# Slots of the first experts named by one-hot matmuls, rows gathered by token and results added into x

## What is computed

```
h = layernorm(x) * (1 + ca) + sa ;  x = x + ga * mamba(h)                 # layer 0, state-space scan
h = layernorm(x) * (1 + cb) + sb
w, idx = top_k(h @ Wr, 2) ;  w = softmax(w)                               # 8 experts, no capacity limit
x = x + gb * sum_k w_k * (silu(h @ W1[idx_k]) * (h @ W3[idx_k])) @ W2[idx_k]
h = ... ;  x = x + ga' * attention(h)                                     # layer 1, 8 heads, causal
h = ... ;  x = x + gb' * experts1(h)                                      # 16 experts, top 2, capacity 640
```

## Time and profile before

| | us |
|---|---|
| median of 3 runs | 3121.29 (3119.28 to 3121.49) |
| the profiled execution | 3119.1 |
| its span, first to last instruction | 3117.0 |
| TensorE busy | 2633.4 (84%) |
| VectorE busy | 2089.7 (67%) |
| GpSimd (POOL) busy | 1148.6 (37%) |
| ScalarE busy | 1157.2 (37%) |

### The profile page before, as it was taken

One profiled execution on the slowest core, in us unless ns is written; L12 is line 12 of the kernel. 1 busy time (PEld: TensorE's weight loads), 2 busy tenths in 40 slices (PEclk: granted clock), 3 DMA queues, 4 the chain that ended last, 5 costly groups with the idle time before them and its releaser, 6 DMA issues. The chain is left out here.

```text
span 3117.0 us, 37717 instructions
## 1 busy us (share of the span) xinstructions
PE 2633.4 (84%) x11376; PEld 1725.6 (55%) x11377; DVE 2089.7 (67%) x4427; ACT 1157.2 (37%) x2271; POOL 1148.6 (37%) x494
## 2 busy tenths in 40 slices
PE   6788888888877508999399999999999999929998
PEld 3233333343333505777267767766777777727776
DVE  4999999999998501222377758784777577535554
ACT  4556566656643202222133413341344143201111
POOL 1798898898896160000210001020102000224444
PEclk8899999999998558999699999999999999959999
DMA  4455555654553522111300000010000000024553
GB/s 152 170 165 166 181 171 153 188 174 150 188 182 108 208 95 88 59 60 57 114 21 8 1 18 18 1 35 22 15 1 28 14 1 1 28 97 110 130 129 69
DMA packets 148491, 278.70 MB, mean 89 GB/s; under 512 B 16060, under 2 KB 101868, under 8 KB 147692
## 3 DMA queue, kind: packets, MB, share of 16 engines
q1 hardware_dynamic: 127052, 238.85, 24.0%
q0 software_dynamic: 20736, 35.80, 5.1%
q10 hardware_dynamic: 544, 2.10, 0.2%
HBM read 210.03 MB, written 62.47 MB: 87 GB/s over the span
## 5 line engine op out<-in xcount | busy, mean ns | idle before, releaser
L678 POOL TENSOR_TENSOR dbx<-u,b_all 128x2048 f32<-128x2048 f32 x128 | 578.3, 4532 | 105.5 <-DVE u L752 51.6
L418 PE MATMUL y_ps<-hc,ident 128*128 128x512 f32 x768 | 403.7, 642 | 119.8 <-DVE hc L832 118.9
L571 ACT ACTIVATE da_ps<-delta,a_neg 128x512 f32<-128x512 f32 x512 | 346.2, 688 | 322.8 <-DVE hc L832 316.9
L1577 POOL DMA_INDIRECT at_y<-outs,slot_of x64 | 63.0, 984 | 820.3 <-DVE x L1862 457.9
L1822 ACT COPY at_pt<-at_pt_ps 128x512 f32<-128x512 f32 (+3 forms) x384 | 171.3, 481 | 505.5 <-PE at_pt_ps L1712 504.1
L418 PEld LDWEIGHTS y_ps<-hc,ident 128*128 128x128 f32 x768 | 139.4, 198 | 346.8 <-DVE hc L832 250.9
L1608 POOL DMA_INDIRECT slots<-at_r_rows,slot_of x64 | 64.3, 1004 | 672.9 <-DVE slot_of L1960 654.6
L1724 PE MATMUL at_o_ps<-at_pt,at_v 128*128 128x128 f32 x2304 | 299.9, 276 | 2.9 <-DVE at_attn L2034 2.9
L1701 PE MATMUL at_s_ps<-at_qk 128*128 128x512 f32 (+3 forms) x768 | 292.4, 491 | 5.0 <-DVE at_v L2010 3.1
L1724 PEld LDWEIGHTS at_o_ps<-at_pt,at_v 128*128 128x128 f32 x2304 | 277.5, 192 | 11.6 <-issue 11.3
L1812 ACT ACTIVATE at_probs<-at_s_ps,at_small 128x128 f32<-128x128 f32 (+7 forms) x256 | 191.5, 748 | 232.6 <-DVE at_small L2021 232.4
(11 more groups left out here) (291 smaller groups left out, 4659.3 us busy)
## 6 DMA issues: line engine op xcount, KB each, us to landing
b_all<-bc_rows SPq DMA_DIRECT2D x128, 512.0 KB, 4.6
c_all<-bc_rows SPq DMA_DIRECT2D x128, 512.0 KB, 5.2
e_w<-L_ffn_w SPq DMA_DIRECT2D x32, 512.0 KB, 5.3
slots<-zeros SPq DMA_DIRECT2D x40, 260.0 KB, 6.1
e_xs<-slots SPq DMA_DIRECT2D x16, 650.0 KB, 7.2
slots<-zeros SPq DMA_DIRECT2D x24, 384.0 KB, 6.3
w<-L_ffn_W SPq DMA_DIRECT2D x24, 384.0 KB, 8.9
e_xs<-slots SPq DMA_DIRECT2D x72, 128.0 KB, 2.0
```

The costliest lines, as they stand in the source:

```text
L418: mm = nc.tensor.matmul(y_ps[par][:], sh.ident[:], hc[:, at % RING_H, :], start=False, stop=last)
L571: nc.scalar.activation(da_ps[s % RING_DA][:], delta[:, c % 2, m, :], ACT.Exp, scale=sh.a_neg[:, m, n:n + 1]).then_inc(S["da_ready"], 1)
L678: nc.gpsimd.tensor_tensor(dbx[:, at % RING_DBX], pair, rows, ALU.mult).then_inc(S["dbx_ready"], 1)
```

## The change

Routing no longer moves rows to slots. The normalised rows are stored to DRAM by token (`rows0`, 4096 rows of 256 values and four numbers: token number plus one, two weights, first expert). To know which token sits in each slot, the kernel builds one-hot matrices from the slot number: its lane (slot modulo 128) and its tile (slot divided by 128, 72 of them), the latter multiplied by the token number. The sum over tokens of lane x tile products is a matmul, whose result is a 128 x 72 table of tokens. The first experts gather their rows with this table, scale the result by weight and gate, and add it to x in DRAM (`sums0`), where the mamba phase has stored x. The attention loads x back. Its constants are loaded during the first experts. `slots0`, `outs0`, their zero fills (24 pieces of 384 KB) and the attention's fetches and combines are gone; 24 tiles' combine work leaves the attention's loops, 8 tiles' leaves its start.

```diff
 # mamba, SP
-                rows, n, tiles = (d["slots0"], g, 3) if g < FILL0 // 3 else (d["slots1"], g - FILL0 // 3, 2)
+            def store_x(c):
+                sp.wait_ge(S["out_added"], (c + 1) * 2)
+                sp.dma_start(rows, sh.x[:, c * CT:(c + 1) * CT]).then_inc(sh.x_stored, 16)
+                    if c and i == GC - 3:
+                        store_x(c - 1)
             ...
+            store_x(CHUNKS - 1)          # last instruction of SP in the phase
 # routing, SP
-                    sp.dma_start(h_rows[:, bass.ds(b * TPB + th * CT, CT), :], row8[...])
+                    rows = d["rows0"][bass.ds(b * T + th * CH, CH), 0:E].rearrange("(j p) e -> p j e", p=P)
+                    sp.dma_start(rows, row8[:, th * CT:(th + 1) * CT, :]).then_inc(rows_copied[th], 16)
             ...                          # after the expert weights
+            sp.wait_ge(meta_ready, 1)
+                sp.dma_start(d["rows0"][:, E:].rearrange("(t p) c -> p t c", p=P), meta[:]).then_inc(meta_stored, 16)
 # routing, POOL
-            for i in range(TILES):
-                for k in range(2):
-                    nc.gpsimd.indirect_dma_start(out=d["slots0"], ..., in_=h_rows[:, i, :], in_offset=None)
+            for b in range(B):
+                pool.wait_ge(block_hot, b + 1)
+                nc.gpsimd.tensor_tensor(hot_block[:, b % 2], hot_block[:, b % 2], of_token(b), ALU.mult).then_inc(block_set, 1)
 # routing, PE
+            for b in range(B):
+                pe.wait_ge(lane_hot, b + 1)
+                pe.wait_ge(block_set, b + 1)
+                for k in range(2):
+                    for j in range(TPB):
+                        last = nc.tensor.matmul(held_ps[:], hot_lane[:, b % 2, k, j, :], hot_block[:, b % 2, k, j, :], ...)
+                last.then_inc(held_done, 1)
 # routing, VectorE (after the slots; four operations turn slot into lane_of and block_of)
+            for b in range(B):
+                if b >= 2:
+                    dve.wait_ge(held_done, b - 1)
+                nc.vector.tensor_tensor(hot_block[:, b % 2], wide(block_of, b, TILES0), every(block_at, TILES0), ALU.is_equal)
+                nc.vector.tensor_tensor(hot_lane[:, b % 2], wide(lane_of, b, P), every(lane, P), ALU.is_equal)
+            dve.wait_ge(held_done, B)    # then eight operations on 128x72: gather_i, add_i, later
 # first experts, POOL
+            def gather(j):
+                if j >= U:
+                    pool.wait_ge(x_turned, j - U + 1)
+                    pool.wait_ge(weight_chain, 2 * (j - U + 1))
+                nc.gpsimd.indirect_dma_start(out=xs[:, j % U, :], out_offset=None, in_=d["rows0"], in_offset=...gather_i[:, j:j + 1])
+            def add(j):
+                pool.wait_ge(y_copied, j + 1)
+                if j:
+                    pool.wait_ge(added, j * 16)
+                nc.gpsimd.indirect_dma_start(out=d["sums0"], out_offset=...add_i[:, j:j + 1], in_=ys[:, j % U, :],
+                                             in_offset=None, compute_op=ALU.add).then_inc(added, 16)
+            AHEAD, BEHIND = 3, 3
+            for j in range(TILES0 + BEHIND):
+                if j + AHEAD < TILES0:
+                    gather(j + AHEAD)
+                if j >= BEHIND:
+                    add(j - BEHIND)
 # first experts, VectorE: body of tile j
                 multiply(j, r)
+                read_weight(j, r, q)     # 2 operations on 128x1
+                gate_rows(j, r)          # 3 chained operations on 128x256
+                if exists(j - 2):
+                    scale_y(j - 2, (r - 2) % U)   # frees y_ps; waits for added of tile j - 6
 # first experts, ScalarE: copy_y is gone
 # first experts, SP: after the first gather has landed, loads of mods (two), gate weights, positions, output weights
 # attention, SP
+                sp.dma_start(sh.x[:, at], d["sums0"][th * CH:(th + 1) * CH, :]...).then_inc(x_first[th], 16)   # two halves of batch 0
+                sp.dma_start(sh.x[:, b * TPB:(b + 1) * TPB], rows_in).then_inc(S["x_in"], 16)                  # batches 1 to 3
 # attention, POOL: fetch is gone.  VectorE: combine becomes stats (a wait and bn_stats)
```

More of the change, by code:

```diff
@@ L36 @@
 TILES0 = SLOTS0 // P
+META = 4
+ROW = E + META
 HEADS, DH = 8, 128
@@ L952, in _ @@
                 sp.dma_start(sh.w2_0[:, e], d["L0_ffn_W2"][e].rearrange("(m p) f -> p m f", p=P)).then_inc(sh.e0_w_in, 16)
+            sp.wait_ge(meta_ready, 1)
+            with nc.allow_non_contiguous_dma(reason="four numbers a row"):
+                sp.dma_start(d["rows0"][:, E:].rearrange("(t p) c -> p t c", p=P), meta[:]).then_inc(meta_stored, 16)
+            for th in range(CPB):
+                sp.wait_ge(rows_copied[th], 16 * B + 1)
+            sp.wait_ge(meta_stored, 16)
         @block.gpsimd
@@ L1033, in _ @@
             nc.tensor.matmul(tot_ps[:], ones[:], both[:], start=True, stop=True).then_inc(ranked, 1)
+            for b in range(B):
[3 more added lines that the diff above has]
+                    for j in range(TPB):
+                        last = nc.tensor.matmul(held_ps[:], hot_lane[:, b % 2, k, j, :], hot_block[:, b % 2, k, j, :],
+                                                start=(b == 0 and k == 0 and j == 0), stop=(b == B - 1 and k == 1 and j == TPB - 1))
+                last.then_inc(held_done, 1)
         @block.vector
@@ L1123, in phase_experts0, with tiles @@
         assert TILES0 % U == 0
-        def tiles(eng, body):
-            for r in range(U):
-                body(r, r, 0)
-            with eng.Fori(1, LOOPS - 1) as q:
+        def tiles(eng, body, apart=1):
+            for j in range(apart * U):
+                body(j, j % U, j // U)
+            with eng.Fori(apart, LOOPS - 1) as q:
                 for r in range(U):
@@ L1243, in body @@
                     copy_x(j + 1, (r + 1) % U)
-                if exists(j - 2):
-                    copy_y(j - 2, (r - 2) % U, q - (1 if r < 2 else 0))
-            for r in range(U):
-                act.sem_inc(y_out[r], 1)
             copy_x(0, 0)
             tiles(act, body)
-            copy_y(TILES0 - 2, U - 2, LOOPS - 1)
-            copy_y(TILES0 - 1, U - 1, LOOPS - 1)
         @block.vector
@@ L1266, in multiply, with read_weight, gate_rows, scale_y @@
                 nc.vector.tensor_tensor(prod[:, r % 2], act_h[:, r % 2], g_ps[r % 2][:], ALU.mult).then_inc(prod_done, 1)
+            def read_weight(j, r, q):
+                dve.wait_ge(x_in[r], q * 16 + 16)
+                if not early(j, U):
+                    dve.wait_ge(y_copied, j - U + 1)
+                at = weight[:, r:r + 1]
+                nc.vector.scalar_tensor_tensor(out=at, in0=xs[:, r, E + 3:E + 4], scalar=sh.owner[:, bass.ds(j, 1)], in1=xs[:, r, E + 1:E + 2],
+                                               op0=ALU.is_equal, op1=ALU.mult).then_inc(weight_chain, 1)
+                dve.wait_ge(weight_chain, j * 2 + 1)
+                nc.vector.tensor_tensor(at, at, xs[:, r, E + 2:E + 3], ALU.add).then_inc(weight_chain, 1)
+            def gate_rows(j, r):
+                for b in range(1, B):
+                    before = sh.mods[:, 2, 0, :] if b == 1 else gate_row[:, r, :]
+                    if b > 1:
+                        dve.wait_ge(gate_chain, j * (B - 1) + b - 1)
+                    nc.vector.scalar_tensor_tensor(out=gate_row[:, r, :], in0=sh.mods[:, 1, b, :], scalar=sh.later[:, b - 1, bass.ds(j, 1)], in1=before,
+                                                   op0=ALU.mult, op1=ALU.add).then_inc(gate_chain, 1)
+            def scale_y(j, r):
+                dve.wait_ge(y_done, j + 1)
+                dve.wait_ge(gate_chain, (j + 1) * (B - 1))
+                dve.wait_ge(weight_chain, (j + 1) * 2)
+                if not early(j, U):
+                    dve.wait_ge(added, (j - U + 1) * 16)
+                nc.vector.scalar_tensor_tensor(out=ys[:, r], in0=y_ps[:], scalar=weight[:, r:r + 1], in1=gate_row[:, r, :],
+                                               op0=ALU.mult, op1=ALU.mult).then_inc(y_copied, 1)
             def body(j, r, q):
@@ L1611, in _ @@
             for b in range(B):
-                if b + 1 < B:
-                    for j in range(TPB):
-                        fetch((b + 1) * TPB + j)
                 if b > 0:
```

232 lines of the change are left out of this document (121 added, 111 removed).

## The result

The change made the kernel faster: 3043.3 us (median of four runs, 3041.4 to 3044.7) against 3120.3 us of the kernel before beside it (3116.1 to 3121.5). The ratio is 0.9755, 95% interval 0.9738 to 0.9772. I had said 3095 with a range of 3036 to 3130: the direction and the range held, the size did not, 77 us against 25. The profiled execution spans 3039.7 us.

| point | before | forecast | after |
|---|---|---|---|
| first experts' first instruction | 1169.22 | 1114.9 | 1115.31 |
| TensorE's first matmul there | 1180.08 | 1120.9 | 1123.37 |
| first accumulating add issued | | 1138.5 | 1140.39 |
| last add issued | | 1507.7 | 1467.43 |
| attention's first instruction | 1509.45 | 1517.0 | 1476.98 |

What follows compares the result with a forecast made beforehand. Two seams, POOL's routing scatters and the gap before the attention, were the bound. From 3119.1 us, 7.6 more up to the attention, 27.3 less at its start and 5.9 less in its loops gave 3093.5, said as 3095, range 3036 to 3130.

Steps and rivals of the forecast that it cites:

- Bound and seams: Routing's 64 POOL scatters and the gap before the attention's first row are the bound that the change attacks.
- Routing: Routing phase: token table ready at 1111.4, 2 us for stores, 1.5 for the phase change, first experts start at 1114.9.
- my 28.4: One-hot work in routing: VectorE's compares and POOL's multiplies one after the other, plus last matmuls, 28.4 us; 18.5 in parallel.
- rival (d): Routing: the store of four numbers a token is the wall, ending at 1131, 20 us more, 3115 us; chance 6%.
- The loop: First experts: the chain of accumulating adds, 5.20 us a tile over TensorE's 4.42, sets the phase; attention starts at 1517.0.
- Their cycle: First experts, one add to the next: issue 1.56, DMA start 0.50, DMA work 1.30, next start 1.84, together 5.20 us.
- 1.84: First experts: from an add's DMA activity ending to the next add's start, 1.36 - 0.29 + 0.77 us.
- (a): First experts: an add's start is hidden in the wait, cycle 4.72 us, 34 us less, 3061 us; chance 23%.
- (b): First experts: landing is quick enough that TensorE or VectorE keeps the pace, about 4.45 us, 3042 us; chance 11%.
- Rival (c): First experts: the gather on POOL's queue delays the adds, cycle 5.75 us, 39 us more, 3134 us; chance 17%.
- VectorE in the loop: First experts: VectorE needs 4.3 us a tile, up to 5.0, just inside TensorE's 4.42.
- Attention's loops: Attention: 24 combines leave VectorE and count only where TensorE waits, at most 5.9 us gained over three batches.

Runs made afterwards that it cites:

- experiment 5: Changed kernel with the one-hot table in bf16, the token number in two parts multiplied in by ScalarE instead of POOL: 3028.6 us.
- experiment 2: Changed kernel with odd tiles' adds into a second tensor, not added up: 3030.4 us; or with plain scatters, still chained, into an unread tensor: 3025.7 us.
- experiment 3: Changed kernel with a POOL memset of 640, 1 or 1120 elements between the wait and each add: 3054.6, 3049.2 and 3084.8 us.
- experiment 4: Changed kernel with the attention's weights loaded behind the third gather: 3046.7 us; or with its constants loaded in the attention again: 3049.8 us.
- experiment 1: Changed kernel with the attention's four old VectorE operations a tile on scratch data: 3061.7 us; or with the old row gathers, unread: 3049.7 us.

## Why the prediction was right and wrong

**Bound and seams: right.** The two gaps that I read in the earlier trace rows went, and their sizes hold to 3 us: the experts start at 1115.3 (1114.9), the attention's first row comes 9.4 us after its first instruction (9.7), and from the end of the last add's issue to the attention it is 8.0 us (7.7). The DMA use that I gave as 18% is 0.19 in the earlier trace rows; nothing hangs on it.

**Routing: right in the end, wrong inside.** The errors cancel: the one-hot work took 4.8 us more than my 28.4, and against that stand a start 1.6 us earlier, 2 us allowed for the stores that were not needed, and some tenths in the rest. VectorE and POOL do block each other: POOL's multiply, begun beside a comparison, took 4.09 us, where the row of 2048 elements gives 2.54, and the comparison that began beside it took 3.27 in place of 1.36. That is the case that no row of before showed, POOL coming second, and it agrees with the Trainium skill ("SBUF — State Buffer", Who interferes with whom: the later one blocks). But that did not set the pace: in the first two batches the multiplies start 5.38 us apart, and TensorE needs 6.9 us a batch, since a record of the earlier trace rows is half an fp32 matmul. The 33.2 us are 5.7 until TensorE's first matmul and 27.55 of TensorE's. In experiment 5, with the matmuls cheap and POOL out of the way, the table takes 17 us. The store of 4096 pieces, rival (d), landed 12.1 us after its issue at 1073.1, long before the table.

**The loop: the step that failed.** "Their cycle: ... Sum: 1.56 + 0.50 + 1.30 + 1.84 = 5.20 us." It measured 4.61. In windows of a quarter of a microsecond the last terms can be read in the changed kernel, between the add issued at 1458.44 and the next at 1463.01 (the DMA share is the last column but one):

```profile
1460.25:1460.50 0.25, 0.00 (x0) 0.00 (x0) 0.00 (x0) 0.00 (x0) 0.00 (x0) 0.50 0.00 0
1460.50:1460.75 0.25, 0.00 (x0) 0.00 (x0) 0.00 (x0) 0.00 (x0) 0.00 (x0) 0.50 1.79 66
...
1461.75:1462.00 0.25, 0.00 (x0) 0.00 (x0) 0.00 (x0) 0.00 (x0) 0.00 (x0) 0.50 0.17 21
1462.00:1462.25 0.25, 0.00 (x0) 0.00 (x0) 0.00 (x0) 0.00 (x0) 0.00 (x0) 0.50 0.00 0
```

Issue 1.55, then 0.5 until the DMA engines start, 1.5 of their work, and 1.0 until the next add starts. The terms 1.56 and 0.50 were right, 1.30 was 0.2 too small, and 1.84 was 0.8 too large. I had built it from 1.36 us between the end of a plain scatter's transfer and POOL's next DMA, took off 0.29 for a plain start and put on 0.77 for an accumulating one. But the 1.36 already held a full start: experiments 2 and 3 show that an indirect DMA that waited for a landing starts 0.7 to 0.8 us after it, plain or accumulating (2.4 to 3.17 us in the plain chain, 3.8 to 4.6 in the accumulating one), and in the kernel before the scatter of the earlier trace rows landed 2.5 us after its start, 0.85 us ahead of POOL's next DMA. The 0.29 belonged to a start after an engine's release. So 0.77 - 0.29 = 0.48 us of one start was counted twice; the other 0.36 us lie in the 1.36 itself, where the changed kernel shows 1.0. The difference, 71 x 0.59 = 42 us, is most of the error of 52.

That the chain sets the phase and a longer step is passed on whole was right, and experiment 3 shows it: at 5.13 us the phase is 39.2 us longer and the kernel takes 3084.8. My rivals (a) at 4.72 us and 3061, and (b), the pace of TensorE and 3042, lay on either side of what came. (a)'s step is the nearest, but its reason, a start hidden in the wait, is not what happens: the start is paid, once. The time is (b)'s, but its mechanism is not: the chain still set the end of the phase, with a lag of 0.19 us a tile over TensorE's 4.42, and cost 15.7 us. That 3042 and 3043 meet is luck: a step of 4.61 us with the rest of my forecast gives 3095 - 42 = 3053, and the attention's loops gave most of what is missing. Rival (c), the gather in the way of the adds, is out: the tail, where there are no gathers, has about the same step (4.4 to 4.6). Large loads in the way of an add do cost what they hold up (experiment 4).

On the landing the Trainium skill ("DMA: Bandwidth & Descriptors", Anatomy of one DMA) gives a fit of about 2.0 us and the bytes at 436 GB/s, an estimate of 2.3 us for the add's 128 KB. It counts the setup in, so by it an add should land 2.3 us after its issue starts. The plain scatters of experiment 2, of the same size, agree with it (2.4 us); the adds, at 3.8 us, do not. Accumulation costs the 1.4 us between them.

**VectorE in the loop: right in kind.** I had 4.3 us a tile; its busy time is 152.61 / 220 of 4.4, or 3.1 us. The busy time leaves out the gaps between chained operations, which my 4.3 held. VectorE was never the bound.

**Attention's loops: too small.** "Three batches: 5.9 us at most." It was 19.5, all or nearly all of it VectorE's (experiment 1). I priced it by TensorE's idle time in one window of 80 us a batch. That window leaves out the batch's seam: from 1840 to 1952 TensorE idled 7.45 us, against 1.95 from 1860 to 1940. Over the four batches the windows show 12 us less idle time of TensorE after the change (39.9 us against 51.8) and also 8 us less busy time for the same matmuls (1125.2 against 1133.5). The second part I had not priced at all, and it lies where the clock was down. These are the sums over the stretches of the four batches with a granted clock of 0.50, the 1.2 GHz level, five before and four after:

```profile
sum 33.05, PE 26.09 PEld 13.18 DVE 18.40 ACT 5.65 POOL 4.38; mean PE 5.22 PEld 2.63 DVE 3.68 ACT 1.13 POOL 0.88
```

```profile
sum 23.48, PE 17.66 PEld 9.86 DVE 14.16 ACT 6.53 POOL 0.00; mean PE 4.41 PEld 2.46 DVE 3.54 ACT 1.63 POOL 0.00
```

Outside them TensorE is busy for 1107 us in both kernels. Before one such fall of the clock, at 1859.44, TensorE had worked 3.38 of 6.84 us. In experiment 1 the clock was at the lower level for 37.1 us with the four operations and for 24.5 us with the fetches, so the stretches come back with VectorE's work; that they come from TensorE's waits for it is my reading, and how the 8 us divide between slower matmuls and matmuls held back is open. "At most" had no ground.

**The sum.** 42 us of the step and 13.6 us of the loops make 55.8; small terms of the other sign (the first add 1.9 us late, the second experts 1.5 us longer, 0.9 us more between the last store and them) bring it to within 1 us of the 52 measured.

## What to carry to other kernels

When DMAs must follow each other, look for one pair of issues in the trace that did wait for each other and take its whole distance; a cycle put together from pieces of other waits can count an end or a start twice, as mine did. Then compare it with the pace of the engine beside it: buffers hide a chain that is a little slower, and the lag comes out as a tail at the end, here 3 adds. When work leaves an engine that feeds TensorE, read TensorE's idle time over whole batches, seams included, and the time at the lower clock level beside it. And before a table is built in fp32, ask whether its numbers can be split into parts that bf16 holds exactly.

## What the hardware showed that I had not expected

- An indirect DMA that stands at a wait for another DMA starts 0.7 to 0.8 us after that one has landed; a memset in its place starts at about 0.1 us. A 0.63 us memset between the two hides all but 0.16 us of the start, a 0.10 us one leaves 0.55 to 0.60.
- Accumulating 128 rows of 1 KB costs 0.61 us more to issue than plain ones (1.59 against 0.98) and lands 1.4 us later from the issue's start (3.8 against 2.4).
- An fp32 matmul of 128x128 by 72 columns has two records of 0.215 us at the 1.2 GHz level; the bf16 one of 144 columns took 2.08 / 16 = 0.13 us, one record.
- POOL's two-input multiply began beside VectorE's two-input comparison and was held: 4.09 us for 1152 elements, ending 2.0 us after the comparison.
- In the attention's four batches the granted clock was 0.50 for 33.1 us before and 23.5 us after VectorE's four operations a tile left its loops.
